# The convolution's input rows: six transfers a batch in place of eight

## The reference

```python
# layer 0
residual = x
h = _bn(x, bn1_gamma, bn1_beta, bn1_mean, bn1_var)
h = conv_general_dilated(h, plk_filter, window_strides=(1, 1), padding=[(8, 8), (8, 8)], feature_group_count=C)
h = einsum('bchw,dc->bdhw', h, pw_weight)
h = gelu(_bn(h, bn2_gamma, bn2_beta, bn2_mean, bn2_var))
a = sigmoid(relu(h.mean(axis=(2, 3)) @ se_w1.T + se_b1) @ se_w2.T + se_b2)
x = residual + gamma * h * a[:, :, None, None]
# layer 1: layer norm over channels, then for both directions
#   x, z = split(x_seq @ W_in); x = silu(causal_conv(x)); dt, B, C from x @ W_xproj
#   h = exp(dt * A) * h + dt * B * x; y = <h, C> + D * x; out += (y * silu(z)) @ W_out
```

## Time and profile before

| | us |
|---|---|
| median of three runs | 5559.85 |
| lowest and highest | 5557.4, 5569.05 |
| the profiled execution, its own time | 5567.16 |
| its span (first to last record) | 5565.3 |
| end of the convolution block (next block's first transfer) | 358.77 |
| mean granted clock of TensorE, share of full speed | 0.818 |

### The profile page before, as it was taken

The page is one execution under the profiler, slowest core; times in us unless marked ns, Lnnn a source line. Parts: engine busy times, 40 slices in busy tenths (PEclk is TensorE's granted clock), DMA queues, the critical chain, the costliest instruction groups (busy, mean ns, idle before and its releaser), DMA issues. The chain is left out here.

```text
span 5565.3 us, 77050 instructions
## 1 busy us (share of the span) xinstructions
PE 4537.5 (82%) x18064; PEld 1235.1 (22%) x18064; DVE 5198.8 (93%) x3757; ACT 3300.4 (59%) x5416; POOL 4820.8 (87%) x2295
## 2 busy tenths in 40 slices
PE   5878578878888888888888888888888888888887
PEld 4553111111222112122111212211122211112222
DVE  5556489999999999999999999999999999999998
ACT  1237556656666666666666666666666666666665
POOL 0020189999999999999999999999999999999998
PEclk9999777777888888888888888888888888888887
DMA  2237555565666666666666666666666666666666
GB/s 75 75 94 235 171 168 183 186 199 191 210 195 195 200 208 208 200 206 198 195 201 209 204 202 203 198 196 201 213 198 208 197 200 198 202 214 195 211 196 203
DMA packets 365956, 1062.76 MB, mean 191 GB/s; under 512 B 71396, under 2 KB 119926, under 8 KB 315340
## 3 DMA queue, kind: packets, MB, share of 16 engines
q1 hardware_dynamic: 355724, 1045.89, 58.2%
q10 hardware_dynamic: 8064, 14.16, 0.8%
q0 software_dynamic: 1984, 1.06, 0.1%
HBM read 849.20 MB, written 211.63 MB: 191 GB/s over the span
## 5 line engine op out<-in xcount | busy, mean ns | idle before, releaser
L1476 POOL TENSOR_TENSOR hc<-hring,c_rep 128x1024 f32<-128x1024 f32 x1541 | 3604.2, 2364 | 82.0 <-DVE hring L1431 78.8
L1431 DVE TENSOR_TENSOR_SCAN hring<-decay,carry,u_ps 128x1024 f32<-128x1024 f32 x1157 | 2670.3, 2331 | 0.0
L1413 DVE TENSOR_TENSOR u_ps<-u_ps,u_rep 128x1024 f32<-128x1024 f32 x1157 | 1396.4, 1207 | 86.0 <-DMA u_rep<-u_scr 65.0
L1171 PE MATMUL u_ps<-stack_b,w_spread 48*128 48x512 bf16 x2314 | 856.0, 455 | 717.6 <-DVE hring L1431 713.2
L1303 ACT ACTIVATE decay<-dt_rep,w_a 128x1024 f32<-128x1024 f32 x1158 | 1325.5, 1145 | 122.4 <-DVE hring L1431 108.9
L1189 PE MATMUL y_ps<-hc,w_gather 128*32 128x512 f32 x6144 | 1036.9, 754 | 0.0
L1303 ACT ACTIVATE u_ps<-dt_rep,w_a 128x1024 f32<-128x1024 f32 x386 | 430.6, 1116 | 1008.4 <-DVE hring L1431 1004.4
L1463 POOL TENSOR_TENSOR drive_p<-u_rep,b_rep 128x1024 f32<-128x1024 f32 x386 | 912.3, 2364 | 12.1 <-DMA u_rep<-u_scr 12.1
L1431 DVE TENSOR_TENSOR_SCAN hring<-u_ps,carry,drive_p 128x1024 f32<-128x1024 f32 x385 | 900.5, 2339 | 0.0
L1171 PEld LDWEIGHTS u_ps<-stack_b,w_spread 48*128 48x128 bf16 x2314 | 134.2, 98 | 1915.2 <-DVE hring L1431 1601.8
L1212 PE MATMUL prep_ps<-xn,w_conv 128*128 128x512 f32 x792 | 459.5, 694 | 121.9 <-ACT xc L1326 95.9
(11 more groups left out here) (152 smaller groups left out, 4398.6 us busy)
## 6 DMA issues: line engine op xcount, KB each, us to landing
dt_rep<-dt_scr SPq DMA_DIRECT2D x194, 1024.0 KB, 5.9
u_rep<-u_scr SPq DMA_DIRECT2D x194, 1024.0 KB, 6.3
c_rep<-bc_scr SPq DMA_DIRECT2D x260, 512.0 KB, 4.7
b_rep<-bc_scr SPq DMA_DIRECT2D x130, 512.0 KB, 5.8
xn<-xn_scr SPq DMA_DIRECT2D x132, 384.0 KB, 5.3
y_scr<-y_sb SPq DMA_DIRECT2D x768, 64.0 KB, 1.9
xn<-xn_scr SPq DMA_DIRECT2D x132, 256.0 KB, 4.7
dt_scr<-dt_sb SPq DMA_DIRECT2D x260, 128.0 KB, 2.1
```

The source lines that it names most:

```text
L1171: mm = nc.tensor.matmul(u_ps[nv % NSLOT][:, sl], w["spread"][:, q, :], upper(stack_b[drv][:, sl]), start=True, stop=True)
L1413: nc.vector.tensor_tensor(slot[:, :], slot[:, :], u_rep[r][:, b, :], ALU.mult).then_inc(drive_ready, 1)
L1431: nc.vector.tensor_tensor_scan(hring[nv % NHR][:, ::step], factor[:, ::step], term[:, ::step], carry[:, drv, nv:nv + 1], ALU.mult, ALU.add ...
L1476: nc.gpsimd.tensor_tensor(hc[nv % NHC][:, :], hring[nv % NHR][:, :], c_rep[q][:, :], ALU.mult).then_inc(c_applied, 1)
```

## The change

`load` is written anew. The view of `x_cols` is now `r (c b x)`, 128 rows, without a dimension for the parity. For each parity a, the chip's side is the 32 partitions from 32 a on. One transfer (line 200 of the changed kernel) brings two groups at once, groups 1 and 3 for parity 0 and groups 0 and 2 for parity 1. Its source is 64 consecutive rows, and both sides are walked as 32 rows, 2 groups, 1024 numbers (256 KB). Another (its line 202) brings 32 rows of one more group (128 KB), group 2 for parity 0 and group 1 for parity 1. What is left is group 0 of parity 0 and group 3 of parity 1, 24 rows each (96 KB, its lines 203 and 204), where the halo is cut off. `X_DMAS` is 6 in place of 8. The total is 960 KB as before. Nothing else differs.

The transfer of parity 0 also writes eight rows of group 3 that lie outside the image (rows 64 to 71 of the flat view are the first rows of the other parity), and that of parity 1 eight such rows of group 0. `batch_norm` multiplies these rows by a scale of 0 and adds a shift of 0 (columns 0 and 2 of `scale` and `shift`), as it did with the zeros.

```diff
--- before.py
+++ after.py
@@ -173,7 +173,7 @@
 
         NCONST = 3 + 3 + 4
 
-        X_DMAS = 2 + 2 * 3
+        X_DMAS = 2 * 3
 
         with nc.Block() as block:
             @block.sync
@@ -184,25 +184,24 @@
                 sp.dma_start(masks[:, :], d["split_masks"]).then_inc(const_in, 16)
                 for i, name in enumerate(("gamma", "beta", "mean", "var")):
                     sp.dma_start(bnp[:, i, :], d["bn1_" + name].partition_broadcast(P)).then_inc(const_in, 16)
-                rows = d["x_cols"].rearrange("(a y) c b x -> a y (c b x)", a=2)
+                rows = d["x_cols"].rearrange("r c b x -> r (c b x)")
 
                 def load(buf, at):
 
 
+
                     cols = bass.ds(at, CB * B * XH)
-
-                    def put(p, q, a, lo, n):
-                        sp.dma_start(xraw[buf][p:p + n, q, :], rows[a, lo:lo + n, cols]).then_inc(x_in[buf], 16)
-
-                    put(PAD, 0, 0, 0, ROWS)
-                    put(ROWS + PAD, 0, 1, 0, 2 * PAD)
-                    put(ROWS + 3 * PAD, 0, 1, 2 * PAD, PAD)
-                    for q in range(1, NCY - 1):
-                        lo = q * CY - PAD
-                        sp.dma_start(xraw[buf][:, q, :], rows[:, lo:lo + ROWS, cols]).then_inc(x_in[buf], 16)
-                    put(0, NCY - 1, 0, H - ROWS + PAD, 2 * PAD)
-                    put(2 * PAD, NCY - 1, 0, H - PAD, PAD)
-                    put(ROWS - PAD, NCY - 1, 1, H - ROWS, ROWS)
+                    n = ROWS - PAD
+                    for a in range(2):
+                        to = xraw[buf][ROWS * a:ROWS * (a + 1), :, :]
+
+                        q0, q1 = 1 - a, 2 - a
+                        first = H * a + q0 * CY - PAD
+                        sp.dma_start(to[:, q0:NCY:2, :], rows[first:first + 2 * ROWS, cols].rearrange("(q y) n -> y q n", q=2)).then_inc(x_in[buf], 16)
+                        first = H * a + q1 * CY - PAD
+                        sp.dma_start(to[:, q1, :], rows[first:first + ROWS, cols]).then_inc(x_in[buf], 16)
+                    sp.dma_start(xraw[buf][PAD:ROWS, 0, :], rows[0:n, cols]).then_inc(x_in[buf], 16)
+                    sp.dma_start(xraw[buf][ROWS:ROWS + n, NCY - 1, :], rows[2 * H - n:2 * H, cols]).then_inc(x_in[buf], 16)
 
                 sp.wait_ge(raw_zero, 1)
                 for i in range(2):
```

## The result

The changed kernel took 5473.73 us (median of four runs, 5473.45 to 5477.1), beside 5563.49 us for the kernel before (four runs, 5557.4 to 5569.05): a ratio of 0.984, 95% interval 0.9823 to 0.9857. The profiled execution took 5477.10 us with a span of 5475.3, which is 90.0 us less than the span before; forecast were 89.9. (The forecast of 5470 us was taken from the median of three runs, 5559.85; with the fourth run it became 5563.49.)

The account below looks back on a forecast made before the run. Transfers on two DMA engines were taken to bound the convolution. TensorE's start 36.67 + slow clock 1.71 + batches 229.2 + tail 0.2 + 0.5 + 0.57 = 268.9 us in place of 358.8; 5559.85 - 89.9 = 5470 us, range 5461 to 5495.

Parts of the forecast that it names:

- What bounded it: Convolution's input loads: two transfers with outer dimension 2 keep two of 16 DMA engines busy, setting the 13.07 us period.
- slower while the others run too: Two busy DMA engines: 581,632 bytes at 52 GB/s take 11.2 us; slowing by the others makes 13.07 us full use.
- The transfers' latency: One input load, from `x_ready` until VectorE may go on: 6.5 us, bounds 3.1 and 18.6, before 18.4.
- the 11.4 that are hidden: Convolution loop: a load has two periods less one `batch_norm`, 2 x 9.55 - 7.7 = 11.4 us, before it delays TensorE.
- the rival that had them land one behind the other: Input loads still exposed in part, six transfers landing in turn: 5507 us, some 5505 by the skill; chance 0.08.
- Its other figure, 14.5 us: That rival's load latency, called halfway between the bounds: period 11.1 us, 37 us lost over 24 batches, 5507 us.
- TensorE's pace: Convolution's 24 batches: TensorE sets the pace at 9.55 us each, bounds 9.47 and 10.0, 229.2 us in all.
- The first load: Convolution's start: the load, behind constants landed at 19.08, is there when VectorE is ready; 4.18 us gained, bounds 0 and 4.18.
- The slow start: Convolution's batch 0: TensorE's clock is slow after a long idle time, costing 1.71 us once; later pauses count none.
- The end of the block: After TensorE's last matmul: ScalarE's copy 0.5 us and the barrier 0.57 us, in place of 7.9 us.

Follow-up runs that it names:

- e1: Kernel before, with each of its two parity-led transfers cut into two of 32 rows, one a parity, ten transfers a batch: 5475.11 us, ratio 0.984.
- e10: Kernel before, with its two parity-led transfers issued first of the eight: 5558.77 us, ratio 0.9991.
- e3: Changed kernel, with each of its two 32-row transfers of one group cut into 31 rows and 1 row: 5593.53 us, ratio 1.0053 to the kernel before.
- e9: Kernel before, with only group 2's parity-led transfer cut by parity, and group 1's, still parity-led, issued first of the nine: 5528.19 us, ratio 0.9935.
- e5: Changed kernel, with the last two of the convolution's five cell shifts left out of TensorE's work: 5429.87 us.
- e4: Changed kernel, with all of a batch's input left out in the loop but one transfer of 24 rows: 5473.78 us.
- e11: The changed kernel run once more, nothing changed: 5473.37 us, ratio 0.9837 to the kernel before.
- e6: Changed kernel, with SyncE waiting until the constants have landed before it issues the first load: 5472.01 us.
- e7: Changed kernel, with each of the filter's three 34-row copies loaded as 32 rows and 2 rows: 5466.07 us.

## Why the prediction was right

*What bounded it* was read rightly: two of 16 engines at full use, seen in a share of 0.13 at 52 GB/s. e1 undoes that alone and has the gain; e10 keeps it and has next to none; e3 brings it back in another way, with one engine. That the two are "slower while the others run too", which the prediction needed to get from 11.2 us to 13.07 and didn't show, is borne out by e9.

*The transfers' latency* was put at 6.5 us; e5 shows 7.5, inside the 11.4 that are hidden. e4 shows that nothing of them is left on the path. So the rival that had them land one behind the other is out: its estimate from the Trainium skill ("DMA: Bandwidth & Descriptors", "Anatomy of one DMA") was 14.3 us, by a fit that the section gives for transfers issued by GpSimd, while SyncE issues these. And e1, which cuts each of the two transfers into its two halves of the partitions, loses nothing by it. Its other figure, 14.5 us, was called halfway between the bounds of 3.1 and 18.6; halfway is 10.9, which would still have been hidden, so the 37 us of that rival were put too high for its own reasoning.

*TensorE's pace* was taken as 9.55 us, with bounds of 9.47 and 10.0. It is 9.47, the lower bound: the gap between batches is nil. That is 2.0 us over 24 batches.

*The first load* was the term that failed. Forecast was TensorE's start at 36.67 us, with constants at 19.08 and 4.18 us won. It started at 40.22 (39.79 in e11). The constants landed at 22.43, since the new load, issued behind them, used the engines' idle share: from 12 to 19 us the share was 0.77 where the kernel before had 0.44, and the two engines that carry the filter would have got less, as in e9. I had written that the load "goes behind them", and counted only what that does to the load and not what the load does to them. Of the 4.18 us 0.78 were left (33.14 to 32.36). e6, which holds the load back, undoes it. Putting the load's effect on the constants at nothing was the step that failed.

*The slow start* cost more in this execution than the 1.71 us of before. From 40.22 to 42.80 it is 2.58 us in place of 1.35, and from 42.80 to 53.91 it is 11.11 in place of 9.47, together 2.9: channel 1 came only 4.01 us after channel 0. But that is a matter of the execution and not of the change: in e11, the same kernel, channel 1 came 2.55 us after channel 0 (42.38 to 44.93) and the start cost 1.4 us in all. That it is the clock is read from the lengths alone: the first twelve matmuls took 2.58 us, as the 2.59 at a granted clock of 0.50, while the granted clock in the profile reads 1.00 from 40.22 us on. After the first batch, none of the later slow batches of before came back, as forecast.

*The end of the block* was right: 271.30 - 270.51 = 0.79 us behind TensorE, where 1.07 were forecast, and 7.9 before.

Together: the start 3.55 us and the clock 1.2 us worse, the pace 2.0 us and the end 0.3 us better, so the block ended at 271.3 and not at 268.9 (at 269.4 in e11). The remaining program's 2.5 us less, scatter that no term forecast, made up for it. So the agreement of 89.9 and 90.0 us to a tenth is chance; the pace, which gives 86 of the 90 us (24 batches of 3.6), is not.

## What to carry to other kernels

A DMA share of 2/16 or 1/16 that lasts is the sign to look for. Here a transfer whose outermost dimension had the size 2 ran on two engines though it filled 64 partitions, one of 31 rows ran on one engine, and the filter's 34 rows on two. Cutting the input so that 32 or 24 rows lead was worth 90 us; going from ten transfers to six was worth nothing that could be measured (5475.1 and 5473.7 us). When the fix is in, look at what was cheap because those engines were idle: here it was the constants that are loaded first, and they had the same fault.

## What the runs showed of the hardware that was not expected

How long SyncE takes to issue a transfer depends on what was issued ahead of it, and not only on the transfer. The four batch-norm vectors took 1.77 to 3.39 us each to issue in the changed kernel, and 0.36 to 0.43 in e7, where only the filter ahead of them was spread:

```profile
8.14 1.77 SPq L186 DMA_DIRECT2D bnp<-in_bn_mean  x1
9.95 2.04 SPq L186 DMA_DIRECT2D bnp<-in_bn_var  x1
```

```profile
4.47 0.43 SPq L187 DMA_DIRECT2D bnp<-in_bn_mean  x1
4.94 0.43 SPq L187 DMA_DIRECT2D bnp<-in_bn_var  x1
```

The first fence is of the changed kernel, the second of e7; the second number of a row is the time of the issue alone. A reading that fits is that transfers which wait for two busy engines hold up the issue of those behind them, whatever engines these would use. No row shows the queue itself, so it is not shown. Nor is it the whole of it: in e7 one issue in the midst of the first load, at 6.83 us, still took 1.98 us.

A DMA engine that moves 24 to 26 GB/s while two or fewer are at work got some 12.5 GB/s during other engines' bursts (e9, worked out above), and in the changed kernel's bursts a busy engine has 14 GB/s. Whether it is the memory, the way to it or the order in the queue that halves it wasn't tried and stays open.
